# Degree counts as matmuls over sign rows, with a block of attention weights folded into them

## The reference

```python
deg = jnp.maximum(segment_sum(ones, dst, 50000), 1.0); deg_isqrt = deg ** (-0.5)
x = x + L0(relu(layernorm(x)), deg_isqrt, ...)       # graph convolution: x[src] * norm, summed by dst
x = x + L1(relu(layernorm(x)), src, dst, W, b)       # sage: rsqrt(1 + deg by src), / (1 + deg by dst) ** 1.5
x = x + L2(relu(layernorm(x)), edge_index, ea, ...)  # GATv2, 4 heads: softmax over the edges of a dst, batch norm
x = x + L3(relu(layernorm(x)), src, dst, etype, ...) # three typed (relational) convolutions
```

## Time and profile before

| | us |
|---|---|
| median of 3 runs | 4790.7 |
| the profiled execution, its own time | 4787.5 |
| its span | 4785.6 |
| prepare(), first to last VectorE instruction | 1.2 to 291.9 |
| attention_weights(), likewise | 292.9 to 308.4 |
| plan(), first instruction | 309.1 |
| busy over the span: PE / DVE / ACT / POOL | 76% / 66% / 39% / 60% |

### The profile page before, as it was taken

One profiled execution on the slowest core, in us unless ns is written; L12 is line 12 of the kernel. 1 busy time (PEld: TensorE's weight loads), 2 busy tenths in 40 slices (PEclk: granted clock), 3 DMA queues, 4 the chain that ended last, 5 costly groups with the idle time before them and its releaser, 6 DMA issues. The chain is left out here.

```text
span 4785.6 us, 80337 instructions
## 1 busy us (share of the span) xinstructions
PE 3651.9 (76%) x25224; PEld 3283.8 (69%) x25224; DVE 3147.1 (66%) x7870; ACT 1858.9 (39%) x4840; POOL 2892.7 (60%) x2890
## 2 busy tenths in 40 slices
PE   5720777758887999999659999437888688868888
PEld 5720667657876777777547777317888688868887
DVE  8975677857777777777678888653444344435554
ACT  6846344434444111111058888661222122212222
POOL 0002777747775777777325555457777577757775
PEclk9965787878888999999879999658888888888888
DMA  8015777756775555555323333455665466646655
GB/s 221 20 28 112 168 184 189 188 117 158 160 160 121 126 120 120 120 119 120 60 64 74 73 75 73 106 140 125 137 137 131 106 135 137 136 102 132 136 132 111
DMA packets 1651583, 582.88 MB, mean 122 GB/s; under 512 B 1550647, under 2 KB 1584310, under 8 KB 1650938
## 3 DMA queue, kind: packets, MB, share of 16 engines
q1 hardware_dynamic: 1032662, 323.45, 29.4%
q10 hardware_dynamic: 534468, 170.04, 14.7%
q0 software_dynamic: 84064, 84.64, 8.9%
HBM read 381.77 MB, written 209.21 MB: 123 GB/s over the span
## 5 line engine op out<-in xcount | busy, mean ns | idle before, releaser
L2005 POOL DMA_INDIRECT early<-node_g,src_w x1173 | 1115.9, 951 | 423.5 <-issue 356.5
L2222 POOL DMA_INDIRECT early<-node_g,src_w x782 | 757.9, 969 | 295.2 <-issue 248.2
L1118 POOL DMA_INDIRECT fscat<-node_g,early x392 | 370.6, 945 | 178.3 <-issue 108.5
L2596 PE MATMUL bank<-early,faS 128*128 128x264 f32 x1568 | 374.3, 391 | 80.5 <-DVE early L2719 79.4
L1265 DVE SCALAR_TENSOR_TENSOR fsprods<-bank,fsattx 128x264 f32<-128x264 f32 x784 | 323.2, 430 | 165.6 <-PE bank L1172 65.1
L2596 PEld LDWEIGHTS bank<-early,faS 128*128 128x128 f32 x1568 | 290.1, 191 | 169.4 <-issue 119.5
L2266 PE MATMUL bank<-l0S,l0msg 128*128 128x128 f32 x1568 | 274.4, 355 | 149.0 <-issue 63.1
L2266 PEld LDWEIGHTS bank<-l0S,l0msg 128*128 128x128 f32 x1568 | 264.3, 267 | 156.1 <-issue 103.4
L1207 ACT COPY fscatT<-bank 128x512 f32<-128x512 f32 x112 | 54.1, 535 | 673.5 <-PE bank L1150 673.5
L2047 PE MATMUL bank<-l3S,l3msg 128*128 128x128 f32 x1568 | 232.3, 317 | 104.2 <-issue 59.4
L2047 PE MATMUL bank<-l5S,l5msg 128*128 128x128 f32 x1568 | 237.0, 322 | 97.7 <-issue 63.9
(11 more groups left out here) (383 smaller groups left out, 10016.0 us busy)
## 6 DMA issues: line engine op xcount, KB each, us to landing
edge_h<-early SPq DMA_DIRECT2D x280, 224.0 KB
node_g<-amax ACTq DMA_DIRECT2D x224, 224.0 KB
early<-edge_h SPq DMA_DIRECT2D x168, 256.0 KB
early<-node_g,src_w POOLq DMA_INDIRECT x1955
l0msg<-edge_a ACTq DMA_DIRECT2D x56, 256.0 KB
l0msg<-edge_h SPq DMA_DIRECT2D x56, 256.0 KB
l1msg<-edge_h SPq DMA_DIRECT2D x56, 256.0 KB
alpha<-edge_h SPq DMA_DIRECT2D x56, 256.0 KB
```

The source lines that it names most:

```text
L1118: pool.indirect_dma_start(out=cat[:, s, t, 0:F], out_offset=None, in_=node_g, in_offset=bass.IndirectOffsetOnAxis(ap=src_i[:, col], axis=0 ...
L2005: pool.indirect_dma_start(out=ring[:, n % RING, t, :], out_offset=None, in_=table_in, in_offset=bass.IndirectOffsetOnAxis(ap=src_w[:, n * ...
L2222: pool.indirect_dma_start(out=ring[:, n % RING, t, :], out_offset=None, in_=table_in, in_offset=bass.IndirectOffsetOnAxis(ap=src_w[:, n * ...
L2596: ins = nc.tensor.matmul(bank[g % RING][:, 0:MW], S[:, s, BAND * t + q, :], M[:, s, t + q, :], start=(q == 0), stop=(q == BAND - 1))
```

## The change

1. An index is split by 128 instead of 256: the tile (392 values) and the partition (128). VectorE writes a row of 392 columns per tile and index for the first; the second is the stationary operand of one product of 128 x 392 per tile and index, in `bank[4]`, `bank[5]` and `bank[6]`.
2. ScalarE makes eleven of a step's fourteen partition rows, as signs: Sign(p + 0.5 - digit) is -1 below the digit and +1 from it on, one instruction a row. Products of such rows count "at or after" minus "before". VectorE makes the other three as one-hot rows, which go to `bank[6]`.
3. At the end, one product per index with a matrix of steps (`step`: halves on two diagonals) takes the differences of neighbouring partitions and so gives the degrees in place; `bank[6]` is added for dst. The roots are taken of reciprocals, not the reciprocals of roots.
4. The hardware loops are written out. VectorE's marks of last edges, the edge columns, the sums of weights and the attention weights' arithmetic are put between its steps (after steps 2, 4, 28 and 30); only src and dst rows are turned before the counts, the other two sets after TensorE's step 2.
5. `attention_weights()` is gone: its eleven loads stand in SP's queue after the x rows, its scratch lies in buffers that are free at that time. `filled` is raised after the first three memsets.

The diff, cut to its core (`MID` = 196; the bodies of `weights()` and `bias_rows()` are those of lines 365 to 369 and 2446 to 2472):

```diff
+                MID, BY_SIGN = T // 2, (HS, 4)
+                iota_i = src_w[:, :]; iota_hi = tb("iota_hi", [P, T], bf16)
+                iota_lo = tb("iota_lo", [P, P], bf16); iota_half = tb("iota_half", [P, P], bf16)
...
-                hi = tb("hi", [P, 2, 2, HS, HI], bf16)
-                lo = tb("lo", [P, 2, 2, HS, 256], bf16)
+                hi = tb("hi", [P, 2, 2, HS, T], bf16)
+                lo = tb("lo", [P, 2, 2, HS, P], bf16)
...
                 def _(act):
...
-                    act.wait_ge(cleared, 1)
...
+                    act.wait_ge(digits_ok, 1)
+                    for n in range(NS):
+                        if n >= 2:
+                            act.wait_ge(counted, n - 1)
+                        for j in range(2):
+                            for t in range(BY_SIGN[j]):
+                                g = n * HS + t
+                                ins = A.activation(lo[:, n % 2, j, t, :], iota_half[:, :], ACT.Sign, bias=minus[:, j, g:g + 1], scale=1.0)
+                        ins.then_inc(oh_low, 1)
...
+                    act.wait_ge(counted, NS)
+                    act.wait_ge(types_out, 32)
+                    A.copy(plain[:, :], bank[6][:, 0:T]).then_inc(plain_ok, 1)
+                    for k, (to, of) in enumerate(((norm, inv_cnt), (rs_send, inv[:, 0, :]), (root, inv[:, 1, :]))):
+                        act.wait_ge(root_in, k + 1)
+                        A.activation(to, of, ACT.Sqrt).then_inc(sq_out, 1)
...
                 def _(dve):
...
+                    for j in range(2):
+                        v.tensor_scalar(minus[:, j, :], dig[:, 2 * j + 1, :], -1.0, None, ALU.mult)
+                        v.tensor_scalar(dig[:, 2 * j, :], dig[:, 2 * j, :], float(-MID), None, ALU.add)
+                    v.drain()
+                    v.sem_inc(digits_ok, 1)
+
+                    def one_hots(n):
+                        if n >= 2:
+                            dve.wait_ge(counted, n - 1)
+                        for j in range(2):
                             for t in range(HS):
...
+                                g = n * HS + t
+                                ins = v.tensor_scalar(hi[:, n % 2, j, t, :], iota_hi[:, :], dig[:, 2 * j, g:g + 1], None, ALU.is_equal)
+                                if t >= BY_SIGN[j]:
+                                    ins = v.tensor_scalar(lo[:, n % 2, j, t, :], iota_lo[:, :], dig[:, 2 * j + 1, g:g + 1], None, ALU.is_equal)
+                        ins.then_inc(oh, 1)
...
+                    for n in range(NS):
+                        one_hots(n)
+                        if n == 2:
+                            last_edges()
+                        if n == 4:
+                            edge_columns()
+                        if n == NS // 2:
+                            weights()
+                        if n == NS // 2 + 2:
+                            bias_rows()
+                    dve.wait_ge(counted, NS)
                     for j in range(2):
-                        ins = v.tensor_copy(hist[:, j, :], bank[4 + j][0:R, :])
+                        ins = v.tensor_copy(signs[:, j, :], bank[4 + j][:, 0:T])
                     ins.then_inc(hist_ok, 1)
...
+                    v.tensor_tensor(cnt[:, :], bank[1][:, 0:T], plain[:, :], ALU.add)
+                    v.drain()
+                    v.tensor_scalar(sums[:, 0, :], cnt[:, :], 1.0, None, ALU.max)
+                    v.tensor_scalar(sums[:, 1, :], bank[0][:, 0:T], 1.0, None, ALU.add)
+                    v.tensor_scalar(sums[:, 2, :], cnt[:, :], 1.0, None, ALU.add)
+                    v.tensor_scalar(no_edge[:, :], cnt[:, :], 0.0, NEG, ALU.is_equal, ALU.mult)
+                    v.drain()
+                    v.reciprocal(inv_cnt[:, :], sums[:, 0, :]).then_inc(root_in, 1)
+                    v.reciprocal(inv[:, 0, :], sums[:, 1, :]).then_inc(root_in, 1)
+                    v.reciprocal(inv[:, 1, :], sums[:, 2, :]).then_inc(root_in, 1)
+                    dve.wait_ge(sq_out, 3)
+                    v.tensor_tensor(upd_scale[:, :], root[:, :], inv[:, 1, :], ALU.mult)
...
                 def _(pe):
...
+                    turns((0, 1))
+                    for n in range(NS):
+                        pe.wait_ge(oh, n + 1)
+                        pe.wait_ge(oh_low, n + 1)
+                        for j in range(2):
                             for t in range(HS):
...
+                                ins = nc.tensor.matmul(to[:, 0:T], lo[:, n % 2, j, t, :], hi[:, n % 2, j, t, :], start=first, stop=last_one)
+                        ins.then_inc(counted, 1)
+                        if n == 2:
+                            pe.wait_ge(put, 1)
+                            turns((2, 3))
                     pe.wait_ge(hist_ok, 1)
                     for j in range(2):
...
+                        ins = nc.tensor.matmul(bank[j][:, 0:T], step[:, :], signs[:, j, :], start=True, stop=True)
                     ins.then_inc(hist_t, 1)
```

More of the change, by code:

```diff
@@ new lines, in prepare @@
+                assert T <= 512
+                iota_i = src_w[:, :]; iota_hi = tb("iota_hi", [P, T], bf16)
+                iota_lo = tb("iota_lo", [P, P], bf16); iota_half = tb("iota_half", [P, P], bf16)
+                flat = lambda ap: ap[:, :, :].rearrange("p a b -> p (a b)")
+                spare = flat(rel_w); weights_at = early[:, 4 * T:8 * T]
+                minus, signs = (flat(amax)[:, 2 * k * T:2 * (k + 1) * T].rearrange("p (j t) -> p j t", j=2) for k in range(2))
+                brb, step, step_b, step_f = spare[:, 0:HF], spare[:, HF:HF + P], spare[:, HF + P:HF + 2 * P], spare[:, HF + 2 * P:HF + 3 * P]
@@ L156, in prepare @@
+                plain = cols(6, 1)[:, 0, :]
                 filled = sm("filled"); raw_in = sm("raw_in"); floats = sm("floats"); sent = sm("sent")
@@ L237, in _ @@
                         act.dma_start(to, of).then_inc(w_in, 16)
-                    act.wait_ge(cleared, 1)
                     A = nc.scalar
[L241 to L258, removed]
+                    act.wait_ge(digits_ok, 1)
[7 more added lines that the diff above has]
+                        ins.then_inc(oh_low, 1)
+                        if n == NS // 3:
+                            act.wait_ge(w_in, 16 * len(loads))
+                            act.sem_inc(w_n, 1)
+                    act.wait_ge(counted, NS)
[4 more added lines that the diff above has]
+                        A.activation(to, of, ACT.Sqrt).then_inc(sq_out, 1)
                 @block.gpsimd
@@ L288, in _ @@
                     v.tensor_scalar(m127[:, 0:1], col_f[:, :], float(P - 1), None, ALU.is_equal)
                     v.tensor_scalar(m127[:, 1:2], col_f[:, :], float(P - 1), -1.0, ALU.not_equal, ALU.mult)
[L290 to L294, removed]
+                    v.tensor_scalar(step[:, :], step_b[:, :], float(P + 1), -0.5, ALU.is_equal, ALU.mult)
@@ L295, in _ @@
                     v.drain()
[L296 to L301, removed]
@@ L334, in _ @@
[L334 to L337, removed]
+                    dve.wait_ge(raw_in, 16 * n_raw)
+                    v.tensor_copy(rows[:, 0:3, :, :].rearrange("r j b p -> r (j b p)"), raw[:, :, :, :].rearrange("r j b p -> r (j b p)")).then_inc(floats, 1)
+                    dve.wait_ge(turned, 1)
+                    v.tensor_copy(src_i[:, 0:T], bank[0][:, 0:T])
+                    v.tensor_copy(dst_i[:, 0:T], bank[1][:, 0:T])
@@ L340, in _ @@
                     ins.then_inc(hist_ok, 1)
+                    dve.wait_ge(types_out, 32)
                     dve.wait_ge(hist_t, 1)
[L342 to L347, removed]
@@ L374, in _ @@
                     pe.wait_ge(floats, 1)
-                    pe.wait_ge(put, 1)
-                    for j in range(4):
-                        for b in range(NBLK):
-                            ins = nc.tensor.transpose(bank[j][:, b * R:(b + 1) * R], rows[:, j, b, :], ident[0:R, 0:R])
-                    ins.then_inc(turned, 1)
-                    pe.wait_ge(cleared, 1)
-                    for j in range(2):
-                        nc.tensor.matmul(bank[4 + j][0:R, :], zb[:, 0:R], zb[:, :], start=True, stop=False)
@@ L394, in _, with turns @@
-                    with nc.tensor.Fori(0, GI) as i:
-                        body(i, False)
-                    for j in range(2):
-                        ins = nc.tensor.matmul(bank[4 + j][0:R, :], zb[:, 0:R], zb[:, :], start=False, stop=True)
-                    ins.then_inc(summed, 1)
+                    def turns(pair):
+                        for j in pair:
+                            for b in range(NBLK):
+                                ins = nc.tensor.transpose(bank[j][:, b * R:(b + 1) * R], rows[:, j, b, :], ident[0:R, 0:R])
+                        ins.then_inc(turned, 1)
```

219 lines of the change are left out of this document (98 added, 121 removed).

## The result

The changed kernel took 4741.56 us (median of 4 runs, 4736.07 to 4746.80), the kernel before 4791.49 beside it (4 runs): a ratio of 0.9897 (95% interval 0.9884 to 0.9909), faster by 1.0%. The forecast was 4739 in a range of 4724 to 4762.

What follows compares the result with a forecast made beforehand. VectorE was taken to set the pace of the degree counts, before and after. Terms -10.2 (start), -31.8 (steps), +12.1 (moved work), -5.2 (tail) and -16.3 (block) sum to -51.4 us off the median 4790.7: 4739, range 4724 to 4762.

Steps and rivals of the forecast that it cites:

- start of the counts (third step): Before the counts: VectorE's third step begins at 29.0 us instead of 39.24, held by ScalarE's weight loads and table load; -10.2.
- 54 steps: Degree counts: VectorE stays the bound and each further step falls from 4.288 to 3.70 us; -31.8.
- work moved into the counts: On VectorE: marks 1.6, edge columns 2.95, sums of weights 1.5 and attention arithmetic 6.05 are not hidden; +12.1 us.
- slow clock behind the pause: TensorE after the 6 us pause in the counts: possibly 1.2 GHz for a step or two, up to 2 us.
- tail: From VectorE's last count row to prepare()'s last product: 16.0 us instead of 21.15; -5.2.
- change of block: Between prepare()'s last instruction and plan(): the handover that remains, 0.93 us.
- The line through 196 and 256 columns: VectorE's compare rows: fixed 0.131 us plus 0.25 ns a column, extended to 0.229 us at 392 columns.
- The rule that the prediction weighed: TensorE: pauses between bursts of matmuls drop the clock to half, which speaks against the change's longer pauses.
- The block's price: Attention weights' own block between prepare() and plan(): 17.2 us gap falls to 0.93 without it; -16.3.
- Slow wide rows: Rival in the counts: 392-column compares cost 0.327 us each, a step 5.16; +27.5 us, 4818; chance 0.05.
- TensorE at 1.2 GHz throughout: Rival in the counts: TensorE stays at half clock after pauses, 4.7 us a step; -5.5 us, 4785; chance 0.06.
- ScalarE as the bound: Rival in the counts: a sign row costs 0.386 us, a step 4.25; -33 us, 4757; chance 0.14.

Runs made afterwards that it cites:

- e4_pool_loads: Against the changed kernel, GpSimd instead of ScalarE issues the weight loads; 4739.35 us in one run, plan() at 258.10 against 262.42.
- e3_sign6: Against the changed kernel, ScalarE makes 13 of a step's 14 partition rows as signs, not 11; 4740.08 us in one run, plan() at 259.45.
- e1_unfold: Against the changed kernel, the attention weights go back to a block of their own behind prepare(); 4749.48 us in one run, plan() at 270.06.

## Why the prediction was right

By its own steps, in the profiled run:

| step | forecast | measured | miss |
|---|---|---|---|
| start of the counts (third step) | 29.0 | 30.93 | +1.9 |
| 54 steps | 3.70 each, 199.8 | 3.73, 201.4 | +1.6 |
| work moved into the counts | 12.1 | 11.8 | -0.3 |
| slow clock behind the pause | 0 (up to 2, in the range) | 1.13 | +1.1 |
| tail | 16.0 | 16.2 | +0.2 |
| change of block | 0.93 | 1.00 | +0.1 |

The 54 steps are what is left of 30.93 to 245.26 without the moved work and the 1.13, so the misses are bound to add up to the whole of -51.4 against -46.8, 4.6; as a check of their own, TensorE's starts at the end of the counts lie 3.73 apart.

- *Start.* The mechanism was right, end to end, and e4_pool_loads shows it: without ScalarE's loads the wait goes. The size was off because the prediction took 19.7, where the loads ended in one run, for fixed. They ended at 21.40 in this run and at 19.61 in the next run of the same kernel, where the third step was at 29.14.
- *Steps.* The line through 196 and 256 columns, 0.229 at 392, held within 0.003 (0.232), outside the widths that it came from. This was the term that carried the gain and the widest bounds. The prediction took its slope from mean durations, 0.25 ns a column. Its own distances between starts, 0.180 and 0.196, give 0.27, so 0.232 for a wide row and 3.74 for a step (an estimate from its own rows): that would have covered the 1.6 us missed here.
- *ScalarE.* 0.294 a row was right (0.292 in e3_sign6, 0.297 to 0.30 here), and so it had time to spare: one row more leaves VectorE the bound, two make ScalarE the bound.
- *Clock.* TensorE fell to the lower level behind the long pause, and twice early on, where it cost VectorE no wait. The rule that the prediction weighed (TensorE: Matmul & The Clock Gate, § Why this matters for your kernels, in the Trainium skill) was right in direction and small here: 1.13 us, since the third step behind the pause took 2.50 again. Pause for pause it didn't hold: the clock fell behind one of 1.93 us and not behind one of 2.55.
- *Tail and block.* Both sums held, 0.2 and 0.1 off. The block's price was tested by e1_unfold; the tail's gain of 5 was read from its rows alone, by no experiment.
- *Rivals.* Slow wide rows: 0.232, no. TensorE at 1.2 GHz throughout: 2.50 in a step of 3.73, no. ScalarE as the bound: not at eleven rows, shown at thirteen.
- *What follows.* It was taken to shift as it is; 4476.4 became 4478.2. Off the profiled runs the total fell by 42.9 (4787.53 to 4744.61), off the medians by 49.9. The kernel's own runs differ by 10, which is more than all the misses together: that the median came within 3 of the forecast is partly luck, and that plan() came within 5 says more. On the clock that the prediction followed, profiled run to profiled run, it was 8.5 short (4736.1 against 4744.61): the 4.6 of the misses, 1.8 of the rest and 2.1 outside the span.

## What to carry to other kernels

Price a new width of an instruction by the distance between starts at two old widths, not by mean durations, and ask first which engine is named behind the bound engine's waits: when that name changes, moving more work the same way costs. Work put on an idle engine need not be free: 5.96 us moved to GpSimd gained 0.2 here, because the engine that sets the pace lost as much. Where a start waits for an engine's DMA issues, try to issue them from another engine. When an edit is worth less than the scatter of the runs, read it at fixed places of the trace, with the stretch behind it as the control.

## What the runs showed of the hardware that was not expected

- *A busy mean is not a cost.* The recorded length of a 392-column row went from 0.32 at 20 us to 0.30 at 154 and 0.46 at 244, its mean is 380 ns, and its distance to the next row stayed 0.23.
- *GpSimd beside VectorE.* Operations on 64 to 800 elements took up to 3.9 us beside VectorE's compares; the same cast of 3 x 264 elements took 0.43, 0.44 and 2.99.
- *The same code varies.* From plan() to the end it took 4465.8 to 4479.6 us over these kernels, with no change in it; what sets that was not looked into.
- *The clock after pauses.* It is not settled by the pause's length alone: in the changed kernel a pause of 2.55 us left matmuls at 14 in 2.50, while 28 behind a pause of 1.93 took 6.66; with the arithmetic on GpSimd 28 behind a pause of 2.50 took 6.25.
